# Fold in banks of its own, its last block and the narrow work among gate and up, down two blocks behind: an AdaLN-FFN pair on one core

## The chip, the cores and the metric

One core of a Trainium2 chip. The metric is the device time of one execution in microseconds; runs of a kernel are compared by their median.

## The reference

For eight blocks x[b] of 128 rows (e) by 512 columns:

```python
y = sum(x[b][:, :length[b]], axis=1) / length[b]          # per row
gate = sigmoid(conv5(y))                                  # along the 128 rows
a = x * gate                                              # each row scaled
h = silu(bitlinear(a, w_gate)) * bitlinear(a, w_up)       # 512 -> 1376
x = x + bitlinear(h, w_down)                              # 1376 -> 512
# bitlinear: rows rounded to int8 by their maximum, weights to -1, 0, 1 by mean |w|
w_eff = codebook_quantised(weight + delta) * scale + delta   # delta = lora_B @ lora_A / 2
c = x @ w_eff.T
x = x + c @ W_base.T + b_base + sum over 4 experts of alpha * (c @ A.T) @ B.T * 2
# alpha = softmax(log(prior) + router logits) over the active experts
```

## The kernel before

Each engine has its own hand-written queue, and semaphores join them. Blocks are numbered 0 to 7; F = 1376 is cut into chunks of 464, 464 and 448 columns.

*Weights of layer 1.* In four row blocks k: `normalise` adds delta, `masks` compares with seven thresholds (L955, VectorE), `codebook` multiplies masks by diagonal steps on TensorE (L660, L661), `value` and `w_eff` (L963, L970, VectorE) finish the block. `fold` (L672) multiplies w_eff by W_base into four banks, so that layer 1 needs one matrix M; `selection` (L642 to L648) gathers the active experts' A and router rows, `last_fold` (L694) multiplies w_eff by them (the narrow fold, 36 columns), `b_rows` (L679) gathers B. `m_high` (L501, ScalarE) and `m_low` (L1107, VectorE) split M into two parts.

*Weights of layer 0.* ScalarE sums absolute values (`weight_sum`, L451), TensorE adds over partitions (`weight_total`, L633), VectorE makes the scale (`weight_scale`, L998 to L1002), ScalarE rounds (`rounded_chunk` L480, `rounded_down` L518), VectorE clips (`ternary`, L1016).

*The gate of layer 0.* `x_sum` (L993, VectorE) for each block, the mean and taps (L1070, L1071), `conv` (L685, TensorE: five shifted matmuls, each in two passes), then exp on ScalarE (L506) and 1/(1 + exp) on VectorE for all eight blocks at once (L1090, L1091). `x_max` (L1020) and `x_scales` (L1079 to L1084) give the quantisation scales for a range of blocks, `x_quantise` (L1098) one block of integers, `x_transposes` (L723) and `x_evacuate` (L495) the operand of TensorE.

*A block.* `gate_up(b, c)` (L756) is eight matmuls into a pair of banks (4 and 5, or 6 and 7, in turn); `silu_chunk` (L528, ScalarE), `hidden_chunk` (L1138 and L1141, VectorE: product and maximum), after three chunks `hidden_scale` (L1145 to L1148), `hidden_round` (L535, ScalarE), `hidden_transposes` (L770), `hidden_evacuate` (L545, L547), `down` (L785, 11 matmuls into bank 2), `residual` (L1153, L1155, VectorE). The new x is transposed into bank 2 again by `x1_transposes` (L792) and split by `x1_high` (L555) and `x1_low` (L1160), after which bank 2 is free for the next down. TensorE's order is the loop

```python
gate_up(b, 0); x1_transposes(b - 2)      # b >= 3
gate_up(b, 1); hidden_transposes(b - 1)  # b >= 1
x_transposes(b + 1)
gate_up(b, 2); down(b - 1)               # b >= 2; down(0) earlier in block 2
```

and the tail: `layer1` groups (L834, 12 matmuls by the two parts of M and of x), the last downs and transposes between them, the router logits (L732 to L734), `z_rows` (L811), the softmax, and `experts` (L841). SP issues all loads in a fixed order, the down weight after the last codebook.

## Time and profile before

| | us |
|---|---|
| runs of the kernel | 160.44, 162.75, 162.95; median 162.75 |
| the profiled execution | 160.56 |
| its span, first to last instruction | 158.8 |
| mean granted TensorE clock | 0.979 |

The profile shows one execution. Starts in it are counted from the first instruction. A matmul's busy time includes its way through the array, so the busy times of neighbours overlap; the distance of their starts is the time that they take.

### The profile page before, as it was taken

The numbers are of one execution on the slowest core, as the hardware profiler recorded it, in microseconds if no ns is written. First come the engines' busy times: TensorE is split into PE (matmuls) and PEld (weight loads), VectorE is DVE, ScalarE is ACT, GpSimd is POOL, SyncE is SP. The second block draws the span as 40 slices with busy tenths as digits, with TensorE's granted clock in tenths as the row PEclk, the third lists the DMA queues.
The fourth block names the chain that finished last, engine by engine and source line by source line (L and its number), as shares of the span: only waits on it lengthen the run. The fifth ranks groups of instructions, "written<-read, shape, count | busy, mean of one in ns | idle before, by whom it ended". The sixth has DMA issues, their size and how long they took to land.

```text
span 158.8 us, 2289 instructions
## 1 busy us (share of the span) xinstructions
PE 146.0 (92%) x755; PEld 90.1 (57%) x762; DVE 114.3 (72%) x306; ACT 96.4 (61%) x160; POOL 3.2 (2%) x17
## 2 busy tenths in 40 slices
PE   6789999999988987597999999999999999999993
PEld 2256575766673444244454555556456857688782
DVE  2799999899699498979999777799777212026461
ACT  3899996968981979987184666767474401500200
POOL 7000000000000000000000000000000000000000
PEclk9999999999985799999999999999999999999999
DMA  5999999479100000000000000000000000000093
GB/s 174 350 405 418 403 418 400 192 261 400 53 0 0 0 0 2 4 0 0 0 4 0 0 0 0 6 0 0 2 0 4 0 0 0 0 4 0 17 378 133
DMA packets 6543, 15.99 MB, mean 101 GB/s; under 512 B 658, under 2 KB 914, under 8 KB 6532
## 3 DMA queue, kind: packets, MB, share of 16 engines
q1 hardware_dynamic: 6532, 15.85, 26.5%
q8 instruction: 6, 0.10, 0.3%
q14 instruction: 5, 0.04, 0.1%
HBM read 13.76 MB, written 2.10 MB: 100 GB/s over the span
## 4 chain that ended last, share of the span: by engine, by line
PE 74%; DVE 11%; ACT 6%; issue 5%; DMA 2%; SPq 0%; ACTq 0%; DVEq 0%
PE bank L756 16%; PE bank L834 14%; PE bank L785 10%; PE bank L672 9%; PE bank L660 4%; PE bank L661 4%; DVE raw_up L1138 3%; DMA cond<-in_cond_w 2%; PE bank L694 2%; PE bank L792 2%; DVE hmax L1141 2%; PE bank L770 2%; ACT tern_d L451 1%; PE bank L841 1%; PE bank L733 1%
## 5 line engine op out<-in xcount | busy, mean ns | idle before, releaser
L756 PE MATMUL bank<-tern_g,l1ab 128*128 128x464 bf16 (+1 forms) x96 | 24.1, 375 | 4.4 <-DVE raw_up L1138 1.7
L756 PE MATMUL bank<-tern_u,l1ab 128*128 128x464 bf16 (+1 forms) x96 | 23.6, 370 | 0.0
L834 PE MATMUL bank<-m_h,fr 128*128 128x512 f32 (+1 forms) x72 | 22.1, 376 | 0.0
L535 ACT ACTIVATE raw_up<-raw_up,hq 128x1376 int16<-128x1376 f32 x8 | 11.5, 1442 | 16.4 <-DVE hq L1148 16.4
L785 PE MATMUL bank<-tern_d,delta 128*128 128x512 bf16 (+1 forms) x81 | 18.8, 379 | 1.6 <-DVE fr L1160 1.0
L528 ACT ACTIVATE cond<-bank,s_g 128x464 f32<-128x464 f32 (+1 forms) x24 | 15.2, 638 | 8.0 <-PE bank L756 7.9
L1138 DVE TENSOR_TENSOR raw_up<-bank,cond 128x464 f32<-128x464 f32 (+1 forms) x24 | 15.2, 632 | 6.1 <-ACT cond L528 5.8
L756 PEld LDWEIGHTS bank<-tern_g,l1ab 128*128 128x128 bf16 x96 | 9.0, 101 | 13.6 <-ACT l1ab L495 4.4
L1141 DVE TENSOR_REDUCE hmax<-raw_up 128x1 f32<-128x464 f32 (+1 forms) x24 | 15.1, 631 | 0.8
L756 PEld LDWEIGHTS bank<-tern_u,l1ab 128*128 128x128 bf16 x96 | 9.8, 102 | 10.2 <-issue 1.6
L785 PEld LDWEIGHTS bank<-tern_d,delta 128*128 128x128 bf16 (+1 forms) x88 | 8.3, 98 | 11.7 <-DVE fr L1160 1.6
L834 PEld LDWEIGHTS bank<-m_h,fr 128*128 128x128 f32 x72 | 13.1, 188 | 2.7
L672 PE MATMUL bank<-wbt,cond 128*128 128x512 f32 x32 | 14.5, 595 | 0.0
L660 PE MATMUL bank<-masks,diag_h 128*128 128x512 f32 x28 | 12.4, 444 | 1.8 <-DVE masks L955 1.8
L834 PE MATMUL bank<-m_l,fr 128*128 128x512 f32 (+1 forms) x36 | 13.3, 369 | 0.0
L955 DVE TENSOR_SCALAR masks<-cond,th 128x512 fp32r<-128x512 f32 x28 | 11.7, 482 | 0.1
L547 ACT ACTIVATE delta<-bank 128x768 bf16<-128x768 int16 (+1 forms) x16 | 11.2, 700 | 0.5 <-PE bank L770 0.5
L661 PE MATMUL bank<-masks,diag_l 128*128 128x512 f32 x28 | 11.0, 395 | 0.0
L1155 DVE SCALAR_TENSOR_TENSOR xs<-bank,s_d,xs 128x512 f32<-128x512 f32 x8 | 6.0, 751 | 5.7 <-PE bank L785 5.5
L555 ACT ACTIVATE fr<-bank 128x512 fp32r<-128x512 f32 x8 | 4.7, 592 | 8.6 <-PE bank L792 8.6
L1160 DVE TENSOR_TENSOR fr<-bank,fr 128x512 fp32r<-128x512 f32 x8 | 5.5, 692 | 5.9 <-ACT fr L555 5.7
L672 PEld LDWEIGHTS bank<-wbt,cond 128*128 128x128 f32 x32 | 6.0, 190 | 6.4 <-issue 6.2
(168 smaller groups left out, 227.1 us busy)
## 6 DMA issues: line engine op xcount, KB each, us to landing
raw_gate<-in_w_gate_t SPq DMA_DIRECT2D x4, 688.0 KB, 8.2
raw_up<-in_w_up_t SPq DMA_DIRECT2D x4, 688.0 KB, 13.8
xs<-in_x SPq DMA_DIRECT2D x8, 256.0 KB, 11.8
...
```

Of the source, the lines that this page charges most:

```text
L528: act.activation(silu[:, n % 2, 0:w], bank_g[n % 2][:, 0:w], ACT.Silu, scale=s_g[:, b:b + 1]).then_inc(silu_done, 1)
L535: act.activation(h_i[:, b % 2, :], hbuf[b % 2], ACT.Copy, scale=hq[:, b:b + 1]).then_inc(hint_done, 1)
L547: act.activation(h_t[:, b % 2, j0:j1, :], src[:, 0:(j1 - j0) * P].rearrange("p (j e) -> p j e", e=P), ACT.Copy).then_inc(ht_done, 1)
L660: pe.matmul(bank_cb[k][:], diag_h[:, t, :], mask[i % SLOTS], start=(n == 0), stop=False)
L661: mm = pe.matmul(bank_cb[k][:], diag_l[:, t, :], mask[i % SLOTS], start=False, stop=(n == NT - 1))
L672: mm = pe.matmul(bank_m[k][:], cond[:, o, k * P:(k + 1) * P], wbt[:, o, :], start=(o == 0), stop=(o == KH - 1))
L756: mm = pe.matmul(dst[:, 0:w], xq_t[:, b % 2, k, :], w_t[:, k, f0:f0 + w], start=(k == 0), stop=(k == KH - 1))
L785: mm = pe.matmul(bank_down[:], h_t[0:rows, b % 2, j, :], tern_d[0:rows, j, :], start=(j == 0), stop=(j == KF - 1))
L834: pe.matmul(bank_y[n_res][:, h0:h1], a[:, b, k, :], m[:, k, h0:h1], start=(n == 0), stop=False)
L955: dve.tensor_scalar(mask[i % SLOTS], cond[:, k, :], t(T_ORDER[n]), None, ALU.is_gt)\
L1138: dve.tensor_tensor(hs, bank_u[n % 2][:, 0:w], silu[:, n % 2, 0:w], ALU.mult)\
L1141: link(dve.tensor_reduce(hmax[:, b % 2, c:c + 1], hs, AX.X, ALU.max, apply_absolute_value=True))
```

## The change

The four fold banks are now 0 to 3, apart from those of gate and up. The last block of the fold is done one bank at a time: bank 0, x transposes of block 0, bank 1, gate_up(0, 0) and (0, 1), banks 2 and 3. Selection stands after gate_up(0, 2), the narrow fold and the total of the down weight after gate_up(1, 2), the b rows in block 2. The banks of M are copied to SBUF (`m_copy`), and split in blocks 5 and 6. The x sums, taps and convolutions are done for blocks 0-1, 2-4 and 5-7 in turn, and the gate is silu(y)/y, with a stand-in where y is all but zero, which needs one table set of ScalarE for all of the layer. x and the x1 transposes leave bank 3 and bank 2 (x: bank 6 once, then the end of bank 1; x1: bank 3). down is two blocks behind gate and up, x1 transposes three. The scale of the residual is computed on GpSimd. The silu of a chunk waits for the gate half only. In TensorE's hidden transposes, eight parts go to the first bank and three to the second instead of six and five.

```diff
+GROUPS = [(0, 2), (2, 5), (5, NB)]
+CONV_WITH_XT = {1: 1, 4: 2}
 ...
+late = slice(HT_LATE * P, HT_LATE * P + H)
+bank_xT = [bank[6][:].bitcast(BF16)[:, 0:H]] + [bank_hT[1][:, late]] * (NB - 1)
+bank_xTi = [bank[6][:].bitcast(I16)[:, 0:H]] + [bank_hTi[1][:, late]] * (NB - 1)
+bank_x1T = bank[3]
+bank_zt = [bank[2], bank[1]]
 ...
-bank_m = [bank[6], bank[7], bank[0], bank[1]]
+bank_m = [bank[0], bank[1], bank[2], bank[3]]
 ...
-bank_delta = [bank[6], bank[7], bank[2], bank[3]]
+bank_delta = [bank[2], bank[3], bank[6], bank[7]]
 ...
-bank_sel = bank[2]
-bank_b = bank[5]
-bank_conv = bank[3][:, 0:NB]
-bank_total = [bank[3][:, 0:KH], bank[3][:, 0:KH], bank[1][:, 0:len(DOWN_PARTS)]]
+bank_sel = bank[3]
+bank_b = bank[3]
+conv0 = (HT_LATE * P + H) // 2
+bank_conv = [bank[6][:, conv0:conv0 + NB], bank[1][:, conv0:conv0 + NB], bank[1][:, conv0:conv0 + NB]]
 ...
-load_x(2)
-load_x(3)
 load_up(0)
 load_wbase(2)
 load_up(1)
+load_up(2)
 load_wbase(3)
-load_up(2)
 load_up(3)
-for b in range(4, NB):
+for b in range(2, 5):
     load_x(b)
 sp.dma_start(l1ab[:], lora1).then_inc(ld_exp, 16)
 sp.dma_start(b_full[3 * ZC:ZS, :], b_base).then_inc(ld_exp, 16)
+for b in range(5, NB):
+    load_x(b)
 ...
+pool.wait_ge(winv_done, 3)
+for b in range(NB):
+    pool.wait_ge(hscale_done, b + 1)
+    pool.tensor_scalar(s_d[:, b:b + 1], harow[:, b:b + 1], w127[:, 2:3], None, ALU.mult).then_inc(sd_done, 1)
 ...
+act.preload_act_table_set("silu_and_others")
 ...
+def conv_out(g):
+    b0, b1 = GROUPS[g]
+    act.wait_ge(conv_ps, g + 1)
+    act.activation(ycond[:, b0:b1], bank_conv[g][:, 0:b1 - b0], ACT.Copy).then_inc(ycond_done, 1)
+def gate_silu(g):
+    b0, b1 = GROUPS[g]
+    act.wait_ge(ysafe_done, g + 1)
+    act.activation(ysilu[:, b0:b1], ysafe[:, b0:b1], ACT.Silu).then_inc(ysilu_done, 1)
+def m_copy(k):
+    act.wait_ge(fold_ps, k + 1)
+    act.activation(m_full[:, k, :], bank_m[k][:], ACT.Copy).then_inc(mfull_done, 1)
 def m_high(k):
-    act.wait_ge(fold_ps, k + 1)
-    act.activation(m_h[:, k, :], bank_m[k][:], ACT.Copy).then_inc(mh_done, 1)
-for k in range(KH):
-    m_high(k)
-act.wait_ge(conv_ps, 1)
-act.activation(yexp[:], bank_conv, ACT.Exp, scale=-1.0).then_inc(yexp_done, 1)
+    act.wait_ge(mfull_done, k + 1)
+    act.activation(m_h[:, k, :], m_full[:, k, :], ACT.Copy).then_inc(mh_done, 1)
+weight_sum_up(0)
+weight_sum_up(1)
+weight_sum_up(2)
+rounded_chunk(0, 0)
+weight_sum_up(3)
+rounded_chunk(0, 1)
+conv_out(0)
+rounded_chunk(0, 2)
+gate_silu(0)
+rounded_chunk(1, 0)
+x_evacuate(0)
+rounded_chunk(1, 1)
+rounded_chunk(1, 2)
 def weight_sum_down(i):
 ...
-act.wait_ge(gu_ps, n + 1)
+act.wait_ge(gate_ps, n + 1)
 ...
+if half == 1 and b + 2 < NB:
+    act.wait_ge(xt_ps, b + 3)
 ...
-for b in range(NB + 2):
+for b in range(NB + 3):
     if b < NB:
         silu_chunk(b, 0)
     if b >= 3:
-        x1_high(b - 2)
-    if b == 0:
-        weight_sum_down(1)
+        x1_high(b - 3)
+    if b == 1:
+        gate_silu(1)
         weight_sum_down(2)
+    if b == 2:
         act.wait_ge(ms_ps, 1)
         act.activation(ms_h, bank_ms[:, 0:KH * ZL].rearrange("p (k c) -> p k c", k=KH),
                        ACT.Copy).then_inc(msh_done, 1)
-    if b == 1:
         rounded_down(0)
     if b < NB:
         silu_chunk(b, 1)
+    if b == 0:
+        weight_sum_down(0)
+        for k in range(KH):
+            m_copy(k)
     if 1 <= b <= NB:
         hidden_evacuate(b - 1)
-    if b + 1 < NB:
+    if 1 <= b < NB - 1:
         x_evacuate(b + 1)
-    if b == 1:
+        if b + 1 in CONV_WITH_XT:
+            conv_out(CONV_WITH_XT[b + 1])
+    if b == 2:
         rounded_down(2)
-    if b == 2:
-        x1_high(0)
     if b < NB:
         silu_chunk(b, 2)
     if b == 0:
+        x_evacuate(1)
+        conv_out(1)
+        weight_sum_down(1)
+    if b == 1:
         weight_sum_down(3)
         weight_sum_down(4)
-    if b == 1:
+    if b == 2:
         rounded_down(3)
         rounded_down(4)
+        act.wait_ge(b_ps, 1)
+        act.wait_ge(rows_done, 5)
+        act.activation(b_full[0:3 * ZC, :], bank_b[0:3 * ZC, :], ACT.Copy,
+                       scale=two_row[0:3 * ZC, :]).then_inc(b_full_done, 1)
+    if b == 3:
+        gate_silu(2)
+    if b in (5, 6):
+        m_high(2 * (b - 5))
+        m_high(2 * (b - 5) + 1)
     if b < NB:
         hidden_round(b)
 for half in range(2):
 ...
+else:
+    pe.wait_ge(sel_read, 2)
 ...
 pe.wait_ge(ld_exp, 32)
+pe.wait_ge(mfull_done, KH)
 ...
-def fold(o):
+def fold(o, k):
-for k in range(KH):
 ...
+mm = pe.matmul(bank_m[k][:], cond[:, o, k * P:(k + 1) * P], wbt[:, o, :],
+               start=(o == 0), stop=(o == KH - 1))
+if o == KH - 1:
+    mm.then_inc(fold_ps, 1)
 ...
 def b_rows():
-    pe.wait_ge(value_done, KH)
+    pe.wait_ge(wtot_read, 3)
 ...
-def conv():
-    pe.wait_ge(ymean_done, 1)
-    pe.wait_ge(wtot_read, 2)
+def conv(g):
+    pe.wait_ge(ymean_done, g + 1)
+    if g == 0:
+        pe.wait_ge(delta_done, KH)
+    b0, b1 = GROUPS[g]
 ...
 lora_delta(2)
 lora_delta(3)
 codebook(1)
-fold(0)
+for k in range(KH):
+    fold(0, k)
 codebook(2)
 weight_total(0, bank_total[0], KH)
-fold(1)
+for k in range(KH):
+    fold(1, k)
 codebook(3)
-fold(2)
+conv(0)
 weight_total(1, bank_total[1], KH)
-for k in range(KH + 1):
-    selection(k)
-b_rows()
-fold(3)
-conv()
+for k in range(KH):
+    fold(2, k)
 def x_transposes(b):
     pe.wait_ge(xq_done, b + 1)
     pe.wait_ge(ident_done, 2)
     if b == 0:
-        pe.wait_ge(yexp_done, 1)
+        pe.wait_ge(ycond_done, 1)
     else:
         pe.wait_ge(xt_done, b)
+    if b == 1:
+        pe.wait_ge(mfull_done, 2)
+    if b in CONV_WITH_XT:
+        conv(CONV_WITH_XT[b])
 ...
 if n == 0:
-    pe.wait_ge(b_full_done, 1)
-if n == 1:
-    pe.wait_ge(ml_done, 2)
+    pe.wait_ge(value_done, KH)
 if n >= 2:
     pe.wait_ge(silu_done, n - 1)
+for k in range(KH):
+    mm = pe.matmul(bank_g[n % 2][:, 0:w], xq_t[:, b % 2, k, :], tern_g[:, k, f0:f0 + w],
+                   start=(k == 0), stop=(k == KH - 1))
+mm.then_inc(gate_ps, 1)
+if n >= 2:
     pe.wait_ge(hmul_done, n - 1)
-for dst, w_t in ((bank_g[n % 2], tern_g), (bank_u[n % 2], tern_u)):
 ...
+for k in range(KH):
+    mm = pe.matmul(bank_u[n % 2][:, 0:w], xq_t[:, b % 2, k, :], tern_u[:, k, f0:f0 + w],
+                   start=(k == 0), stop=(k == KH - 1))
 mm.then_inc(gu_ps, 1)
 ...
 if b == 0:
     pe.wait_ge(msl_done, 1)
 else:
-    pe.wait_ge(x1l_done, b)
+    pe.wait_ge(x1_done, b)
 pe.wait_ge(ht_done, 3 * (b + 1))
 ...
 def x1_transposes(b):
     pe.wait_ge(x1_done, b + 1)
+if b == 0:
+    pe.wait_ge(b_full_done, 1)
+else:
+    pe.wait_ge(x1l_done, b)
 for k in range(KH):
-    mm = pe.transpose(bank_down[:, k * P:(k + 1) * P], xs[:, b, k * P:(k + 1) * P], ident)
+    mm = pe.transpose(bank_x1T[:, k * P:(k + 1) * P], xs[:, b, k * P:(k + 1) * P], ident)
 mm.then_inc(x1t_ps, 1)
 ...
+fold(KH - 1, 0)
+x_transposes(0)
+fold(KH - 1, 1)
 for b in range(NB):
     gate_up(b, 0)
     if b >= 3:
-        x1_transposes(b - 2)
+        x1_transposes(b - 3)
     gate_up(b, 1)
-    if b == 1:
-        pe.wait_ge(ml_done, KH)
-        weight_total(2, bank_total[2], len(DOWN_PARTS))
-    if b == 2:
-        down(0)
+    if b == 0:
+        fold(KH - 1, 2)
+        fold(KH - 1, 3)
     if b >= 1:
         hidden_transposes(b - 1)
-    if b + 1 < NB:
+    if 1 <= b < NB - 1:
         x_transposes(b + 1)
     if b == 2:
-        x1_transposes(0)
+        b_rows()
     gate_up(b, 2)
+    if b == 0:
+        x_transposes(1)
+        for k in range(KH + 1):
+            selection(k)
+    if b == 1:
+        for k in range(KH):
+            last_fold(k)
+        weight_total(2, bank_total[2], len(DOWN_PARTS))
     if b >= 2:
-        down(b - 1)
+        down(b - 2)
 last = NB - 1
 layer1(0)
-x1_transposes(last - 1)
+x1_transposes(last - 2)
+down(last - 1)
 hidden_transposes(last)
 layer1(1)
+x1_transposes(last - 1)
 down(last)
 layer1(2)
 ...
+def y_safe(g):
+    o = slice(*GROUPS[g])
+    dve.wait_ge(ycond_done, g + 1)
+    link(dve.tensor_tensor(ytiny[:, o], ycond[:, o], ycond[:, o], ALU.mult))
+    link(dve.tensor_scalar(ytiny[:, o], ytiny[:, o], TINY_SQUARE, STAND_IN, ALU.is_lt, ALU.mult))
+    dve.tensor_tensor(ysafe[:, o], ycond[:, o], ytiny[:, o], ALU.add).then_inc(ysafe_done, 1)
+    dve.wait_ge(ysafe_done, g + 1)
+    link(dve.reciprocal(yrec[:, o], ysafe[:, o]))
+def gates(g):
+    o = slice(*GROUPS[g])
+    dve.wait_ge(ysilu_done, g + 1)
+    link(dve.tensor_tensor(gate[:, o], ysilu[:, o], yrec[:, o], ALU.mult))
 ...
-dve.tensor_scalar(w127[:, i:i + 1], wscale[:, i:i + 1], 1.0 / QMAX, None, ALU.mult)
+link(dve.tensor_scalar(w127[:, i:i + 1], wscale[:, i:i + 1], 1.0 / QMAX, None, ALU.mult))
 ...
+weight_scale(0, bank_total[0])
 masks(3, 4)
 w_eff(2)
-weight_scale(0, bank_total[0])
 lengths()
-selectors()
 x_sum(0)
+x_sum(1)
+y_taps(0)
 ternary_chunk(0, 0, rounded_by_act=1)
+x_max(0, 2)
+ternary_chunk(0, 1, rounded_by_act=2)
 value(3)
+weight_scale(1, bank_total[1])
+y_safe(0)
+gates(0)
+x_scales(0, 2)
+x_quantise(0)
 w_eff(3)
-dve.wait_ge(lp_done, 1)
-dve.tensor_copy(pr_bc[:], pr.unsqueeze(2).broadcast_to([NE, 2, P])).then_inc(sel_done, 1)
-x_sum(1)
-ternary_chunk(0, 1, rounded_by_act=2)
+ternary_chunk(0, 2, rounded_by_act=3)
+ternary_chunk(1, 0, rounded_by_act=4)
 x_sum(2)
 x_sum(3)
-weight_scale(1, bank_total[1])
-ternary_chunk(0, 2, rounded_by_act=3)
+ternary_chunk(1, 1, rounded_by_act=5)
 x_sum(4)
-x_sum(5)
-dve.wait_ge(sel_ps, 1)
 ...
-ternary_chunk(1, 0, rounded_by_act=4)
-x_sum(6)
-x_sum(7)
 ...
-x_max(0, 1)
-ternary_chunk(1, 1, rounded_by_act=5)
 ...
-dve.wait_ge(yexp_done, 1)
-link(dve.tensor_scalar(yexp[:], yexp[:], 1.0, None, ALU.add))
-link(dve.reciprocal(gate[:], yexp[:]))
-x_scales(0, 1)
 ...
+y_taps(1)
 ...
-dve.tensor_tensor(m_l[:, k, :], bank_m[k][:], m_h[:, k, :].bitcast(F32),
+dve.tensor_tensor(m_l[:, k, :], m_full[:, k, :], m_h[:, k, :].bitcast(F32),
 ...
+dve.wait_ge(gu_ps, n + 1)
 ...
-link(dve.tensor_scalar(s_d[:, o], harow[:, o], w127[:, 2:3], None, ALU.mult))
+dve.wait_ge(sd_done, b + 1)
 ...
-    dve.tensor_tensor(x1t_l[:, b, :, :], bank_down[:].rearrange("p (k e) -> p k e", k=KH),
+    dve.tensor_tensor(x1t_l[:, b, :, :], bank_x1T[:].rearrange("p (k e) -> p k e", k=KH),
                       x1t_h[:, b, :, :].bitcast(F32), ALU.subtract).then_inc(x1l_done, 1)
-for b in range(NB + 2):
-    if b + 1 < NB:
+for b in range(NB + 3):
+    if b == 1:
+        selection_out()
+        y_safe(1)
+    elif b + 1 < NB:
         x_quantise(b + 1)
-    if b == 2:
-        residual(0)
     if b < NB:
         hidden_chunk(b, 0)
     if b == 0:
+        selectors()
+        dve.wait_ge(lp_done, 1)
+        dve.tensor_copy(pr_bc[:], pr.unsqueeze(2).broadcast_to([NE, 2, P])).then_inc(sel_done, 1)
+    if b == 1:
+        gates(1)
+        x_scales(2, 5)
+        x_quantise(2)
+    if b == 2:
+        weight_scale(2, bank_total[2])
         dve.wait_ge(msh_done, 1)
         dve.tensor_tensor(ms_l, bank_ms[:, 0:KH * ZL].rearrange("p (k c) -> p k c", k=KH),
                           ms_h.bitcast(F32), ALU.subtract).then_inc(msl_done, 1)
-    if b == 1:
         ternary_down(0)
     if b >= 3:
-        x1_low(b - 2)
+        x1_low(b - 3)
     if b < NB:
         hidden_chunk(b, 1)
+    if b == 0:
+        x_max(2, 5)
+    if b == 1:
+        x_sum(5)
     if b == 2:
-        x1_low(0)
-        x_scales(4, 6)
-    if b == 1:
         ternary_down(1)
         ternary_down(2)
     if b < NB:
         hidden_chunk(b, 2)
         hidden_scale(b)
-    if b == 0:
-        x_max(5, 6)
-        weight_scale(2, bank_total[2])
     if b == 1:
+        x_sum(6)
+        x_sum(7)
+        y_taps(2)
+    if b == 2:
         ternary_down(3)
         ternary_down(4)
-        x_max(4, 5)
-    if 2 <= b <= NB:
-        residual(b - 1)
-    if b == 2:
-        x_max(6, NB)
-        x_scales(6, NB)
-    if b == 5:
+        x_max(5, 7)
+    if b == 3:
+        y_safe(2)
+        x_max(7, NB)
+        gates(2)
+        x_scales(5, NB)
+    if 2 <= b <= NB + 1:
+        residual(b - 2)
+    if b in (5, 6):
+        m_low(2 * (b - 5))
+        m_low(2 * (b - 5) + 1)
+    if b == 7:
         stacked_b()
```

## Rows read from the trace of the kernel before

**Rows 1.** The page: its span, and busy us (share) xinstructions of each engine.
```profile
span 158.8 us, 2289 instructions
...
PE 146.0 (92%) x755; PEld 90.1 (57%) x762; DVE 114.3 (72%) x306; ACT 96.4 (61%) x160; POOL 3.2 (2%) x17
```

**Rows 2.** Busy time by stretch: stretch, us, busy (xcount) per engine, granted clock, DMA.
```profile
34.00:41.80 7.80, 7.80 (x34) 4.92 (x33) 7.45 (x24) 5.76 (x5) 0.00 (x0) 1.00 0.85 313
41.80:46.60 4.80, 4.80 (x47) 4.79 (x45) 3.49 (x13) 4.54 (x8) 0.00 (x0) 1.00 0.00 0
46.60:53.40 6.80, 5.45 (x18) 2.12 (x16) 6.26 (x14) 3.04 (x4) 0.00 (x0) 0.50 0.00 0
53.40:65.00 11.60, 8.50 (x57) 4.53 (x54) 8.86 (x22) 10.70 (x21) 0.00 (x0) 1.00 0.00 1
65.00:78.00 13.00, 11.29 (x64) 5.64 (x66) 11.36 (x29) 8.77 (x13) 0.00 (x0) 1.00 0.00 1
78.00:95.70 17.70, 17.34 (x108) 9.38 (x109) 15.12 (x37) 11.04 (x18) 0.00 (x0) 1.00 0.00 1
95.70:121.20 25.50, 25.12 (x156) 13.74 (x158) 20.76 (x47) 16.04 (x26) 0.00 (x0) 1.00 0.01 2
```

**Rows 3.** The chain that ended last, TensorE's pieces: start us, us, what.
```profile
31.01 3.43 PE bank L672 x8
34.56 0.25 PE bank L642 x2
...
37.50 1.03 PE bank L679 x2
...
41.97 1.01 PE bank L685 x10
42.98 3.60 PE bank L694 x32
...
48.24 3.27 PE bank L756 x8
...
87.15 1.57 PE bank L756 x8
88.74 0.66 PE bank L792 x4
...
90.96 0.61 PE bank L770 x11
91.58 0.22 PE bank L723 x4
...
93.36 2.32 PE bank L785 x10
95.69 1.57 PE bank L756 x8
```

**Rows 4.** Timeline of ScalarE: start us, us, line, operation [idle before, releaser].
```profile
30.78 3.51 ACT L480 ACTIVATE tern_i<-raw_gate,winv 128x1856 int16<-128x1856 f32 x2
...
51.53 0.65 ACT L528 ACTIVATE cond<-bank,s_g 128x464 f32<-128x464 f32 x1 [3.43 <-PE bank L756]
...
61.06 1.56 ACT L518 ACTIVATE tern_i<-raw_down,winv 128x1536 int16<-128x1536 f32 x1
```

**Rows 5.** Timeline of VectorE, same columns.
```profile
25.27 1.27 DVE L955 TENSOR_SCALAR masks<-cond,th 128x512 fp32r<-128x512 f32 x3
...
79.55 1.21 DVE L1020 TENSOR_REDUCE rmax<-xs 128x2 f32<-128x1024 f32 x1
80.80 0.16 DVE L1079 TENSOR_TENSOR arow<-rmax,gate 128x2 f32<-128x2 f32 x1
...
81.86 0.55 DVE L1098 TENSOR_SCALAR head_sb<-xs,gate,qx 128x512 int16<-128x512 f32 x1
82.32 0.63 DVE L1138 TENSOR_TENSOR raw_up<-bank,cond 128x464 f32<-128x464 f32 x1
...
83.66 0.69 DVE L1160 TENSOR_TENSOR fr<-bank,fr 128x512 fp32r<-128x512 f32 x1
```

More of the change, by code:

```diff
@@ L538, in hidden_evacuate @@
             def hidden_evacuate(b):
-                for half, (j0, j1) in enumerate(((0, 6), (6, KF - 1))):
+                for half, (j0, j1) in enumerate(((0, HT_EARLY), (HT_EARLY, KF - 1))):
                     act.wait_ge(ht_ps, 2 * b + half + 1)
@@ L761, in hidden_transposes @@
                 pe.wait_ge(hint_done, b + 1)
[L762 removed]
+                for half, (j0, j1) in enumerate(((0, HT_EARLY), (HT_EARLY, KF))):
                     if b == 0:
[L764 to L765 removed]
+                        pe.wait_ge(mfull_done, 2)
                     else:
```

136 lines of the change are left out of this document (62 added, 74 removed).

## The prediction

> **What bounds the kernel now.** I read the page first [rows 1]: TensorE is busy for 92% of a span of 158.8 us, so what can be won is mostly the time in which it waits or runs slowly. The busy times by stretch [rows 2] say where that is. From 95.7 to 121.2 us TensorE works 25.12 of 25.50 us and VectorE 20.76: there TensorE sets the pace. From 53.4 to 78 us it is idle for 3.1 + 1.71 us, and VectorE is as full (20.22 of 24.6 us): there TensorE waits for hidden chunks, quantised x and the ternary down weight. From 46.6 to 53.4 us the granted clock is 0.50, the lower level of 1.2 GHz, after 4.8 us in which TensorE did only narrow matmuls (8 and 36 columns), and it is idle for 1.35 us besides.
>
> The chain gives the price of each piece of TensorE's work [rows 3]: eight matmuls of a gate_up chunk 1.57 us (3.27 at the lower clock), down 2.32, hidden transposes 0.61, x transposes 0.22, x1 transposes 0.66, a fold of one block 3.43 (0.86 for one bank), one convolution 1.01, narrow fold 3.60, selection 2.94 (from 34.56 to 37.50), b rows 1.03. A block costs 8.54 us (from 87.15 to 95.69) when nothing waits.
>
> **What could be won.** From 31 us to the start of block 5 (95.69) TensorE is idle for 1.35 + 3.1 + 1.71 + 0.36 = 6.5 us [rows 2], and the lower clock costs 3.27 - 1.57 = 1.7 us on the first gate_up chunk and some 1.1 on the second [rows 3]: 9.3 us in all. The change moves the last fold, selection, narrow fold and b rows into this stretch, but doesn't shorten them. It adds two convolutions: ten matmuls each for three or fewer columns instead of eight. Below nothing they cannot be; the weight loads, not the columns, make their length, so I take the 1.01 us of the wide one for each (bounds 0.3 and 1.3), 2.0 us of new TensorE work.
>
> **The walk, block by block.** I lay the new order of each queue on the durations of before.
>
> *Up to the first gate_up.* VectorE ends value(2) at 25.27, where the masks start [rows 5]. New order: scale of gate 0.76 (one wait more than now), three masks 1.2, w_eff(2) 0.6, lengths 0.6, two x sums at 0.8, taps 0.3 (the small ones as they stand in the same timeline): 30.3. Ternary 0.55 and x maxima of two blocks 1.25 (79.55 to 80.80 [rows 5]): 32.1. ScalarE now also loads its silu table early (1.28 us), which pushes back its first rounded chunk from a start that waited for the weight scale to one that no longer does: it starts at 27.75 as it does now, so the load is free. The second rounded chunk ends at 32.6 as now (two of them take 3.51 from 30.78 [rows 4]). Then ternary 0.55, value(3) 0.66, scale of up 0.76, y_safe 0.8 (four small linked operations), gate 0.2, x_scales 1.06, x_quantise 0.46 [rows 5], and only then w_eff(3): 37.8. TensorE has done codebook(3) at 31.0, conv(0), the weight total and fold(2) at 35.7 [rows 3] and waits 2.2 us for w_eff(3). Fold, x transposes, evacuation (0.5): the first gate_up starts at 39.9 instead of 48.24. The second waits for a ternary chunk whose rounding ScalarE could begin only after the evacuation: 42.2, a stall of 0.75. The third rounded chunk of up ends at 43.1, and the first silu starts there, against 51.53 [rows 4]. So the head start is 8.4 us.
>
> *Block 0.* VectorE: quantise 0.46, three hidden chunks at 1.34 (82.32 to 83.66 [rows 5]), selectors and the copy behind them 1.2, maxima of three blocks 1.78, hidden scale 0.77: 51.9. TensorE does two banks of the last fold, gate_up, conv(1), transposes and selection by 51.2. ScalarE has copied the four banks by 47.7, in time for the selection.
>
> *Block 1.* Silu(1,0) stands behind hidden_round(0) on ScalarE, which starts at 51.9: 53.8. Then hidden chunk, gates, x_scales, x_quantise(2): 56.9. TensorE, through with the hidden transposes at 54.9, waits 2.1 us. gate_up(1,2) 58.8, narrow fold 62.4, total of the down weight 62.65. VectorE, with three x sums (2.4) and the taps among its chunks, is at 63.5.
>
> *Block 2.* gate_up(2,0) ends at 64.2, hidden chunk 65.7, scale of down 66.5 (in the kernel before, rounding of the down weight starts at 61.06 [rows 4]). ScalarE has waited 2.2 us for it. Rounding (1.46), silu, two evacuations, another rounding, silu(2,2): 71.8. VectorE ends that chunk and its scale at 73.9 and the last two ternary parts at 74.5. down(0) could have started at 69.0; it gets its parts at 71.4, 71.8, 74.3 and 74.5 and ends at 75.0 instead of 71.3: 3.7 us of stall.
>
> *Block 3.* Without a stall TensorE is through at 84.3. But VectorE can start hidden chunk (3,2) only at 82.1 (conv(2) stands ahead of its gate_up), and then has chunk 1.31, scale 0.77, y_safe 0.8, a maximum 0.7, gates 0.2, x_scales 1.06 and the residual 0.67 to do: 87.6. The x1 transposes of block 4 wait for that residual from 85.9 to 87.8, 1.9 us, with gate_up(4,1) queued behind them. Block 5 then starts at 94.5; small gaps between groups, which the chain has and this walk lacks, make it 95.05.
>
> **The sum.** That is 0.65 us ahead of 95.69. But down lags by one more block now: TensorE still owes one down and one set of x1 transposes, 2.32 + 0.62 = 2.9 us. From there on TensorE is the bound as before; m_high and m_low (four times 0.5 and 0.6 us) fit into blocks 5 and 6, where VectorE has 8.5 - 6.6 = 1.9 us to spare. The tail has the same pieces in the order x1 transposes, down, hidden transposes, and each wait lies beside a 2.8 us layer-1 group. Net: +2.3 us, a span of 161.1. Checked the other way: new stalls 2.2 + 0.75 + 2.1 + 3.7 + 1.9 = 10.7 us and convolutions 2.0, against 9.3 us of waits and slow clock that go, and 0.6 to 1.6 us of small gaps which those stalls swallow: +1.8 to +2.8.
>
> The profiled execution took 160.56 us for its span of 158.8; with 1.76 around it, 161.1 gives 162.9. The median of the runs is 162.75, two of the three being 2.2 to 2.4 above the profiled one. I add half of that, since I don't know whether what lengthens those is still there, and predict 164.0.
>
> **The clock, and the skill.** The trace has the clock at full through 34 to 41.8 us with selection in it (the profile's TensorE was busy throughout and wide folds followed), and at half after 4.8 us of narrow work alone [rows 2]. In the new order the longest narrow stretch is conv(1), x transposes and selection, 4.2 us, then the narrow fold, 3.6 us behind a stall; I count no fall in the sum. The Trainium skill ("Perfetto Trace Analysis", Matmul Optimizations) says that TensorE scales with its utilization and that matmuls should run back-to-back in batches. By it, narrow work between wide chunks is right, but the thin stretch under down(0) is wrong. The rule gives no price; the rows do, in the first rival.
>
> **Rivals.**
> 1. *The clock falls again*, in selection, in the narrow fold or while down(0) waits for its parts. For: the fall after 4.8 us of narrow work. Against: two stretches are shorter, and TensorE waits at 55 and 86 us anyway, which swallows part. Each chunk costs 1.7 us more; two or three of them, less what is swallowed: +1 to +3.5, a time of about 166.
> 2. *The head start carries through (faster).* VectorE has 5.0 us of idle time in the walk between 43.7 and 87.6 (0.85 in block 1, 0.9 and 1.25 in block 2, 2.0 in block 3), all of it waiting for orders of queues. If silu(1,0) and x_quantise(2) don't hang on hidden_round(0), the narrow fold and the scale of down come 2 us earlier, and down(0) loses its stall; the place is down(0)'s end: if it is before 71 us, the result is faster. All 5.0 us gained give 164.0 - 5.0 = 159.0, and with the slow clock of before gone from the other runs too, 157. Against: each wait stands written in the queues, and VectorE has some 5 us more to do after the first silu than before (x sums, selectors, maxima, gates).
> 3. *The extra idle is narrower than that, and all is even*: stalls of down(0) and block 4 come out at half, 2.8 us less: 161.2, no change to be seen.
>
> **How the numbers follow.** My walk 0.45 (it and rival 3 lie within 2%), rival 3 0.15, clock rival 0.22, head start 0.18. The range takes in half of the head start case and the clock case with its upper price: 158.0 to 168.0. A change of about 2%, 3.3 us, is what a measurement of this kernel can tell from none: faster means under 159.5, slower over 166.0. Faster 0.18 plus a little of rival 3 gives 0.2; slower most of the clock case and the upper part of the walk, 0.27; the rest 0.53.
>
> **What would show it.** Right: first gate_up near 40 us after an idle of some 2 us ended by w_eff; first silu near 43; TensorE idle near 55 to 57 ended by the quantised x; down(0) in pieces, ended by tern_d near 75; an idle of 1 to 2 us before the x1 transposes near 86, ended by VectorE; block 5 starting near 95; busy TensorE after it. Wrong: down(0) in one piece, block 5 starting before 92, a granted clock of 0.50 for over 3 us anywhere after 45, or waits in the tail between the layer-1 groups.

## The result, and the profile after

| | before | after |
|---|---|---|
| runs | 160.44, 160.45, 162.75, 162.95 us; median 161.6 | 166.95, 167.58, 169.26, 169.87 us; median 168.42 |
| ratio after / before | | 1.039, 95% interval 1.031 to 1.047 |
| profiled execution, its span | 160.56, 158.8 us | 166.95, 165.2 us |
| mean granted TensorE clock | 0.979 | 0.959 |

Medians are of all runs; the ratios and their intervals leave out runs more than 1.5% above the fastest of their kernel.

The changed kernel is slower by 3.9%. The forecast was 164.0 with a range of 158.0 to 168.0. That is 0.8% above the 162.75 it started from, and the prediction gave the larger chance, 0.53, to a change too small to be told from none, and 0.27 to a slower kernel. So the direction was right and the size was not: the profiled execution, 166.95, lies near the upper end of the range, the median of the runs 0.4 us above it.

The page of the changed kernel, its first lines:

```profile
span 165.2 us, 2369 instructions
...
PE 151.2 (92%) x775; PEld 94.6 (57%) x782; DVE 114.5 (69%) x308; ACT 99.7 (60%) x169; POOL 5.7 (3%) x25
...
PEclk9999999999997598799999689999999999999999
```

TensorE is busy 5.2 us longer than before (146.0 [rows 1]), VectorE 0.2 us. The clock row has three dents where the kernel before had one. Only TensorE's matmuls stretch with the clock: in the first dent four of them start 1.52 us after the four before (52.57 to 54.09) instead of 0.79 (40.59 to 41.38), while a silu of 464 columns takes ScalarE 0.65 us and a product of them VectorE 0.64 us inside the dent and outside. So the dents are the first thing to follow.

TensorE's timeline of the changed kernel (start us, us, line, operation [idle before, releaser]), the rows at which the walk of the prediction can be checked:

```profile
31.00 1.17 PE L741 MATMUL bank<-ytaps,shifts 128*128 128x2 f32 x10
32.03 0.36 PE L687 MATMUL bank<-wsum,ones 128*128 128x4 f32 x2
...
38.49 1.13 PE L726 MATMUL bank<-wbt,cond 128*128 128x512 f32 x2 [2.55 <-DVE cond L1042]
...
40.59 0.95 PE L808 MATMUL bank<-tern_g,head_sb 128*128 128x464 bf16 x4
...
43.01 0.96 PE L808 MATMUL bank<-tern_g,head_sb 128*128 128x464 bf16 x4 [0.69 <-DVE tern_u L1110]
...
52.57 1.73 PE L808 MATMUL bank<-tern_g,head_sb 128*128 128x464 bf16 x4
...
74.91 1.25 PE L842 MATMUL bank<-tern_d,delta 128*128 128x512 bf16 x5 [1.37 <-DVE tern_d L1110]
77.83 0.82 PE L842 MATMUL bank<-tern_d,delta 128*128 128x512 bf16 x3 [1.66 <-DVE tern_d L1110]
78.49 0.95 PE L808 MATMUL bank<-tern_g,head_sb 128*128 128x464 bf16 x4
...
91.63 0.66 PE L853 MATMUL bank<-shifts,xs 128*128 128x128 f32 x4 [2.03 <-DVE xs L1239]
...
100.09 0.95 PE L808 MATMUL bank<-tern_g,head_sb 128*128 128x464 bf16 x4
```

A convolution of two columns takes 1.03 us (31.00 to 32.03), as the one of eight did (1.01 [rows 3]). The wait for w_eff is there (2.55 us; forecast 2.2), the wait for the ternary chunk (0.69; 0.75), the pieces of down(0) (1.37 + 1.66 us of visible wait; forecast 3.7 from an earlier possible start), the wait of the x1 transposes for the residual (2.03; 1.9). The first gate_up starts at 40.59 instead of 48.24. But block 5 starts at 100.09, where the walk had 95.05. The wait for x of block 2, forecast at 2.1 us, is not there at all: TensorE came too late for it.

The stretches of the changed kernel, columns as in [rows 2]:

```profile
49.00:51.40 2.40, 2.40 (x19) 2.19 (x17) 2.33 (x3) 2.12 (x4) 0.00 (x0) 1.00 0.00 0
51.40:58.30 6.90, 6.90 (x21) 3.39 (x22) 4.21 (x19) 3.86 (x6) 0.00 (x0) 0.51 0.01 2
58.30:65.00 6.70, 6.70 (x61) 5.74 (x60) 5.84 (x17) 5.30 (x10) 0.00 (x0) 1.00 0.00 1
65.00:68.40 3.40, 3.40 (x11) 1.28 (x9) 1.87 (x7) 1.18 (x3) 0.00 (x0) 0.51 0.00 0
68.40:92.30 23.90, 18.73 (x117) 10.38 (x118) 19.11 (x49) 15.74 (x24) 1.35 (x4) 1.00 0.00 1
92.30:95.70 3.40, 3.40 (x16) 1.77 (x15) 2.05 (x4) 1.24 (x2) 0.00 (x0) 0.52 0.00 0
```

Three falls to the lower level of 1.2 GHz: one behind conv(1), x transposes and selection (6.9 us long), one behind the narrow fold (3.4), one behind the 2.03 us wait for the residual (3.4). Half of 13.7 us is 6.8 us of TensorE's work lost. In the kernel before TensorE worked for 5.45 of the 6.80 low microseconds [rows 2], so 2.7 us of its work were lost, and it had waits behind them that could take some of them up; here TensorE is busy for all of the low stretches.

### The profile page after: what moved, and what is told of

Same layout as the page of the kernel before. It is cut to its first block, busy times and chain, and to the rows that moved or that the text cites. A ratio compares the mean times of both kernels' runs of the same rounds, so it can differ in the third digit from the quotient of the medians.

```text
span 165.2 us, 2369 instructions
## 1 busy us (share of the span) xinstructions
PE 151.2 (92%) x775; PEld 94.6 (57%) x782; DVE 114.5 (69%) x308; ACT 99.7 (60%) x169; POOL 5.7 (3%) x25
## 4 chain that ended last, share of the span: by engine, by line
PE 70%; ACT 14%; DVE 10%; issue 5%; ACTq 0%; DVEq 0%
PE bank L895 13%; PE bank L808 11%; PE bank L814 11%; PE bank L842 9%; ACT tern_d L475 6%; PE bank L827 3%; PE bank L853 2%; PE bank L669 2%; ACT tern_i L505 2%; PE bank L749 2%; PE bank L666 2%; PE bank L726 2%; PE bank L902 1%; PE bank L741 1%; PE bank L782 1%
## 5 line engine op out<-in xcount | busy, mean ns | idle before, releaser
L808 PE MATMUL bank<-tern_g,head_sb 128*128 128x464 bf16 (+1 forms) x96 | 25.6, 394 | 0.7 <-DVE tern_u L1110 0.7
L814 PE MATMUL bank<-tern_u,head_sb 128*128 128x464 bf16 (+1 forms) x96 | 25.5, 393 | 0.0
L1222 DVE TENSOR_TENSOR raw_up<-bank,wbt 128x464 f32<-128x464 f32 (+1 forms) x24 | 15.2, 632 | 12.9 <-ACT wbt L568 9.2
L568 ACT ACTIVATE wbt<-bank,s_g 128x464 f32<-128x464 f32 (+1 forms) x24 | 15.3, 641 | 3.6 <-PE bank L808 3.5
L726 PE MATMUL bank<-wbt,cond 128*128 128x512 f32 x32 | 15.0, 603 | 2.6 <-DVE cond L1042 2.6
L814 PEld LDWEIGHTS bank<-tern_u,head_sb 128*128 128x128 bf16 x96 | 10.2, 107 | 11.6 <-issue 3.5
L808 PEld LDWEIGHTS bank<-tern_g,head_sb 128*128 128x128 bf16 x96 | 9.5, 105 | 10.7 <-issue 3.3
L589 ACT ACTIVATE delta<-bank 128x1024 bf16<-128x1024 int16 (+1 forms) x16 | 11.2, 701 | 7.3 <-PE bank L827 7.3
L1330 DVE TENSOR_TENSOR xs<-bank,xs 128x512 f32<-128x512 f32 (+1 forms) x9 | 5.2, 626 | 5.6 <-PE bank L902 5.6
```

The lines of the kernel that those rows point to most:

```text
L568: act.activation(silu[:, n % 2, 0:w], bank_g[n % 2][:, 0:w], ACT.Silu, scale=s_g[:, b:b + 1]).then_inc(silu_done, 1)
L589: act.activation(h_t[:, b % 2, j0:j1, :], src[:, 0:(j1 - j0) * P].rearrange("p (j e) -> p j e", e=P), ACT.Copy).then_inc(ht_done, 1)
L726: mm = pe.matmul(bank_m[k][:], cond[:, o, k * P:(k + 1) * P], wbt[:, o, :], start=(o == 0), stop=(o == KH - 1))
L808: mm = pe.matmul(bank_g[n % 2][:, 0:w], xq_t[:, b % 2, k, :], tern_g[:, k, f0:f0 + w], start=(k == 0), stop=(k == KH - 1))
L814: mm = pe.matmul(bank_u[n % 2][:, 0:w], xq_t[:, b % 2, k, :], tern_u[:, k, f0:f0 + w], start=(k == 0), stop=(k == KH - 1))
L1222: dve.tensor_tensor(hs, bank_u[n % 2][:, 0:w], silu[:, n % 2, 0:w], ALU.mult)\
```

## The experiments

Eleven kernels ran. Each is compared with the kernel before on the same chip, whose medians there were 162.2 to 162.7 us (160.5 to 164.1); so I give ratios beside times. The changed kernel was not run again beside them, so differences from its median of 168.42 are the rougher ones.

**Dense matmuls in three thin stretches.**

```diff
+def dense(dst, n):
+    for i in range(n):
+        pe.matmul(dst[:], warm[:, 0:P], warm[:], start=True, stop=True)
 for k in range(KH + 1):
     selection(k)
+    dense(bank[2], 1)
 ...
 for k in range(KH):
     last_fold(k)
+    dense(bank[3], 1)
 ...
 def x1_transposes(b):
+    if b == 1:
+        pe.wait_ge(x1l_done, 1)
+        dense(bank[3], 8)
     pe.wait_ge(x1_done, b + 1)
```

> The changed kernel with dense matmuls (512 bf16 columns, results unused) put between the narrow ones: one after each of the five selection steps, one after each of the four steps of the narrow fold, eight while TensorE waits for the residual of block 1. They cost 9 x 0.22 = 2.0 us of TensorE's time outside of waits, of which the wait for x of block 2 takes up half. Theory A (the slow clock behind the narrow stretches is what the change costs beyond its walk: three falls, 6.8 us of work lost to half speed, 5.0 after what waits swallow): no fall after 45 us, block 5 starts near 96 instead of 100.1, span near 161.5, 3 to 4 us less than the changed kernel. Theory B (the granted clock falls for reasons that have nothing to do with what TensorE does there, or the orders of the queues alone hold the time): the falls stay and the time is that of the changed kernel plus up to 2 us.

Median 168.02 us, ratio 1.040 (1.030 to 1.050): no gain. Neither theory as written. The falls did not stay where they were, nor go. The profile of this kernel in stretches:

```profile
36.00:39.00 3.00, 0.62 (x2) 0.38 (x3) 2.83 (x11) 1.55 (x1) 0.00 (x0) 1.00 1.05 400
39.50:43.50 4.00, 4.00 (x14) 1.45 (x12) 2.65 (x7) 3.73 (x3) 0.00 (x0) 0.57 0.23 76
...
53.00:57.00 4.00, 4.00 (x15) 1.94 (x15) 0.96 (x6) 2.23 (x4) 0.00 (x0) 0.57 0.02 4
...
73.00:77.00 4.00, 1.96 (x9) 0.51 (x6) 3.78 (x7) 4.00 (x8) 0.00 (x0) 1.00 0.00 0
77.00:84.50 7.50, 5.96 (x18) 2.86 (x19) 5.16 (x12) 3.77 (x5) 0.50 (x1) 0.54 0.01 2
```

The fall behind the residual's wait is gone. New ones stand behind the wait for w_eff(3) (TensorE busy for 0.62 of 3 us before it) and behind the pieces of down(0) (1.96 of 4 us), which the changed kernel's profiled execution had passed at full clock; one comes even behind selection with its five dense matmuls. I call a stretch thin in which TensorE has only narrow matmuls or waits. Over the two profiles the falls stand behind five of them: the wait for w_eff(3), selection, the narrow fold, the pieces of down(0) and the wait for the residual. Which of them brings a fall is not fixed.

**Residual ahead of the gate work of block 3.**

```diff
+if 2 <= b <= NB + 1:
+    residual(b - 2)
 if b == 3:
     y_safe(2)
     x_max(7, NB)
     gates(2)
     x_scales(5, NB)
-if 2 <= b <= NB + 1:
-    residual(b - 2)
```

> The changed kernel with residual(1) ahead of y_safe(2), the last maximum, gates(2) and x_scales(5, 8) on VectorE in block 3. Theory A (x1 transposes of block 4 wait for the residual because 2.9 us of other work stand ahead of it, and the third fall of the clock is the consequence of that wait): the 2.0 us wait at 90 us goes, the third fall with its 1.7 us goes too, minus 3 to 3.7 us. Theory B (what stood ahead of the residual is then late for the next block, since hidden_round(3) and x_quantise(5) wait for it): the wait moves to the hidden transposes of block 4 and the gain is under 1 us.

Median 165.06 us, ratio 1.012 (1.000 to 1.025), 3.4 us under the changed kernel's median. The wait is gone; the x1 transposes of block 4 follow gate_up at once:

```profile
91.68 0.95 PE L808 MATMUL bank<-tern_g,head_sb 128*128 128x464 bf16 x4
92.46 0.95 PE L814 MATMUL bank<-tern_u,head_sb 128*128 128x464 bf16 x4
93.25 0.60 PE L853 MATMUL bank<-shifts,xs 128*128 128x128 f32 x4
```

It did not return at the hidden transposes. Theory A for the wait. The profiled execution had four low stretches (from 9.5, 40, 54 and 77.5 us), none near 92, and took 167.35 us at a mean clock of 0.948, where the changed kernel took 167.58 at 0.949; the best run, 163.00 us, shows 0.979. So the gain of the median seems to go mostly with the clock, and how much of it the third fall is worth isn't shown.

**Scale of the down weight first.**

```diff
+if b == 2:
+    weight_scale(2, bank_total[2])
 if b < NB:
     hidden_chunk(b, 0)
 ...
 if b == 2:
-    weight_scale(2, bank_total[2])
```

> The changed kernel with the scale of the down weight ahead of the first hidden chunk of block 2 on VectorE (it waits there for 1.4 us anyway). Theory A (down(0) waits 3.0 us for its ternary parts because rounding begins at 69.75, 2.9 us after ScalarE was free): rounding begins near 67, down(0) loses 2 to 3 us of wait, block 3 starts at 76 instead of 78.5, and the time falls by 2 us. Theory B (down(0) waits because VectorE and ScalarE are full in block 2 whatever the order): under 0.7 us.

Median 163.45 us, ratio 1.009 (1.003 to 1.014): 5 us under the changed kernel's median, more than twice what theory A gave. The mechanism is as theory A had it, in ScalarE's and then TensorE's timeline:

```profile
66.83 1.58 ACT L558 ACTIVATE tern_i<-raw_down,winv 128x1536 int16<-128x1536 f32 x1 [0.49 <-DVE winv L1096]
```

```profile
72.00 1.25 PE L842 MATMUL bank<-tern_d,delta 128*128 128x512 bf16 x5 [0.28 <-DVE tern_d L1110]
74.91 0.82 PE L842 MATMUL bank<-tern_d,delta 128*128 128x512 bf16 x3 [1.66 <-DVE tern_d L1110]
```

Rounding begins 2.9 us sooner, down(0) ends 2.9 us sooner and waits 1.1 us less. The rest goes with the clock: two low stretches instead of three (51.5 and 89 us), 5.1 us lost instead of 6.8. At nearly the same mean clock the two kernels are 2.3 us apart (164.61 us at 0.958, the changed kernel 166.95 at 0.959; one run each), which is what theory A gave. So a scale of four small operations, moved into an idle gap of VectorE, is worth some 1.4% by itself.

**w_eff of the last block first.**

```diff
 value(3)
+w_eff(3)
 weight_scale(1, bank_total[1])
 ...
 x_quantise(0)
-w_eff(3)
```

> The changed kernel with w_eff(3) right behind value(3) on VectorE instead of behind the quantisation of block 0. Theory A (the first gate and up hang on the chain w_eff, fold, x transposes): the 2.55 us wait at 38.5 becomes one of some 0.5 us for the x transposes, the first gate_up comes 0.9 us sooner. Theory B (by block 5 the waits behind it have swallowed such a lead, as they have swallowed most of the 8 us that the change wins at the first gate_up): the time moves by less than 0.5 us though the lead is there at 40 us.

Median 166.03 us, ratio 1.023 (1.012 to 1.035). The wait of 2.55 us is now one of 1.91 us for the quantised x:

```profile
38.81 0.40 PE L782 MATMUL bank<-ident_b,head_sb 128*128 128x128 bf16 x4 [1.91 <-DVE head_sb L1138]
```

Theory A had 0.5: it forgot that the quantisation itself moves back by w_eff's 0.6. The second gate_up starts at 42.38 instead of 43.01: the lead is 0.63 us. The gain of 2.4 us between medians is more than that lead, and the profiled execution lost 5.1 us to the clock instead of 6.8, so this run can't tell theory B from A: the clock's steps are larger than the effect.

**The three together.**

> The changed kernel with the three reorderings together: w_eff(3) behind value(3), the scale of the down weight ahead of the first hidden chunk of block 2, residual(1) ahead of the gate work of block 3. Theory A (the waits written into the new queues, and the falls of the clock that thin stretches bring, are what the change costs): the single gains add up, about 0.6 + 3.5 + 2 us, a span near 160 and a time level with the kernel before (ratio 0.98 to 1.01). Theory B (they share one cover: each only moves the point at which VectorE holds everything): no more than the best of the three, ratio 1.005 or above.

(The edit is the last three diffs.) Median 160.30 us, ratio 0.988 (0.976 to 1.000). Theory A; the sum of the single gains to the medians (3.4 + 5.0 + 2.4 = 10.8) is not reached (8.1). That they share the clock's part would explain it, but no run shows it. The profiled execution (0.968) still fell behind selection and behind the narrow fold, 5.1 us lost.

**The three with dense matmuls in the narrow stretches.** (Two after each step of selection and of the narrow fold; the edit is that of the first experiment with 2 in place of 1 and without the third place.)

> e5_three with two dense matmuls (512 bf16 columns, results unused) after each step of selection and of the narrow fold: 9 x 2 x 0.22 = 3.9 us of TensorE's time, about 1 us of it inside a wait. Theory A (the narrow stretches bring the falls near 51 and 65 us): these two falls go, worth up to 5 us, so 1 to 2 us below e5_three. Theory B (the falls come from the waits): they stay, and the time is 2 to 3 us above e5_three.

Median 160.92 us, ratio 0.999 (0.994 to 1.004). No fall in the profile (mean clock 1.0, span 159.0); six of the ten runs show 1.0 and take 160.80 to 160.92, the other four 0.989. So the falls of the narrow stretches do go, theory A in the mechanism, but it had 1 to 2 us of gain, and at 3.9 us of added work nothing is won: buying the clock back with idle matmuls costs what it returns here.

**Dense matmuls in every thin stretch, order untouched.**

```diff
+pe.wait_ge(value_done, KH)
+dense(bank[4], 11)
 fold(KH - 1, 0)
 ...
+if b == 0 and j in (3, 8):
+    pe.wait_ge(ht_done, 4)
+    dense(bank[0], 7)
 if b == 0 and j in firsts:
```

(and two after each narrow step, eight before the residual's wait)

> The changed kernel, order untouched, with dense matmuls in every thin stretch: eleven in the wait for w_eff(3), two after each narrow step, seven in each of the two long waits of down(0), eight in the wait for the residual. Outside of waits they cost 3.9 us less the 1 to 2 us that the wait for x of block 2 takes. In the first experiment falls came at 39.5, 53 and 77 us instead of 51, 65 and 92, each behind one of these stretches. Theory A (any of the five thin stretches can bring a fall, which of them do varies from execution to execution, and the total is what they have in common): no fall at all, a span of 161.1 (the walk at full clock) + 2.5 = 163.5, and less spread between runs. Theory B (the clock falls whatever is put there): falls of 3 to 7 us remain and the time is 169 or more.

Median 165.66 us, ratio 1.025 (1.017 to 1.034); three of the four runs lie at 165.47 to 165.70 us with a mean clock of 1.0, the fourth at 169.39 with 0.969. Theory A, and close in numbers: a span of 163.9 us against 163.5. Here, unlike in the kernel with the three reorderings, padding does pay: the median is 2.8 us under the changed kernel's, though the intervals of the two ratios just overlap. The fourth run shows that padding everything doesn't keep every fall away.

This is the measurement that separates the two parts of the loss. TensorE's timeline of this kernel, and one row of ScalarE's:

```profile
38.63 1.12 PE L730 MATMUL bank<-wbt,cond 128*128 128x512 f32 x2 [0.19 <-DVE cond L1056]
...
55.27 0.65 ACT L568 ACTIVATE wbt<-bank,s_g 128x464 f32<-128x464 f32 x1 [0.92 <-PE bank L812]
...
59.38 0.40 PE L786 MATMUL bank<-ident_b,head_sb 128*128 128x128 bf16 x4 [1.19 <-DVE head_sb L1152]
...
92.08 0.66 PE L863 MATMUL bank<-shifts,xs 128*128 128x128 f32 x4 [0.30 <-DVE xs L1253]
...
98.87 0.95 PE L812 MATMUL bank<-tern_g,head_sb 128*128 128x464 bf16 x4
```

The wait for x of block 2 is there again, 1.19 us; the forecast was 2.1. If the missing 0.9 us are dense work that the wait took up, the dense matmuls cost 3.9 - 0.9 = 3.0 us, and without them and without falls the span would be 163.9 - 3.0 = 160.9 us. That estimate leans on the forecast. One from rows alone: the dense matmuls in selection make ScalarE wait 0.92 us for block 1's first gate bank, so the x behind it comes that much later; those in the narrow fold stretch it from 3.72 us in the changed kernel (60.95 to 64.67) to 5.12 (61.13 to 66.25), by 1.4; and the waits that hold the others are still open by 0.15 to 0.40 us, so those cost nothing. That makes 163.9 - 2.3 = 161.6 us. The walk had 161.1, between the two.

It also says what the order is worth by itself. This kernel and the one before it have the same padding in the narrow stretches and differ in the three reorderings; in runs without a fall they take 165.47 to 165.70 and 160.80 to 160.92 us. At full clock the three reorderings are worth 4.8 us.

**The narrow work taken apart.**

```diff
 gate_up(b, 0)
+if b == 1:
+    for k in range(KH + 1):
+        selection(k)
+if b == 2:
+    last_fold(2)
 ...
 gate_up(b, 1)
+if b == 2:
+    last_fold(3)
 ...
 if b == 0:
     x_transposes(1)
-    for k in range(KH + 1):
-        selection(k)
 if b == 1:
-    for k in range(KH):
-        last_fold(k)
+    last_fold(0)
+    last_fold(1)
     weight_total(2, bank_total[2], len(DOWN_PARTS))
```

(on top of the three; VectorE's and ScalarE's copies behind them move to match)

> e5_three with the narrow work taken apart: selection behind gate_up(1,0), so that the convolution and the x transposes don't adjoin it, and the four steps of the narrow fold two behind gate_up(1,2), one behind gate_up(2,0), one behind gate_up(2,1). No work is added. Theory A (what counts is how long the narrow work runs unbroken): fewer or shorter falls before 70 us, 1 to 3 us below e5_three, and below the kernel before. Theory B (the order is worth nothing, the falls are the waits'): the same as e5_three within 1 us.

Median 158.81 us, ratio 0.983 (0.976 to 0.990), all four runs between 158.56 and 159.11: faster than both kernels. Theory A. One low stretch is left, behind a wait of 1.90 us for the quantised x of block 0, and down(0) has only one long wait:

```profile
39.00:43.00 4.00, 4.00 (x11) 1.36 (x10) 3.53 (x11) 4.00 (x4) 0.00 (x0) 0.57 0.33 113
43.00:73.00 30.00, 26.89 (x178) 17.68 (x176) 26.54 (x77) 25.65 (x43) 1.02 (x3) 1.00 0.00 1
73.00:94.00 21.00, 20.83 (x135) 12.09 (x134) 17.33 (x41) 12.34 (x22) 0.62 (x3) 1.00 0.00 1
```

Beside the clock, spreading also lets the total of the down weight go two steps of the narrow fold (1.8 us) sooner. This run doesn't tell the two apart, but the runs of the three together hint at the clock: the one with 0.987 took 158.36 us, no more than the 158.56 to 159.11 here at 0.989, and those with 0.978 and 0.968 took 159.96 to 161.41. The gain would then be that all four runs here keep more of the clock.

**The kernel before with dense matmuls in its narrow fold.**

```diff
 for k in range(KH):
     for o in range(KH):
         mm = pe.matmul(bank_ms[:, k * ZL:(k + 1) * ZL], cond[:, o, k * P:(k + 1) * P],
                        sel_f[:, o, :], start=(o == 0), stop=(o == KH - 1))
+    dense(bank[4], 2)
```

> The kernel before with two dense matmuls (512 bf16 columns, results unused) after each of the four steps of the narrow fold: 8 x 0.22 = 1.7 us of added work on TensorE. In the profile of before the clock is at half from 46.6 to 53.4 us, behind the convolution and the narrow fold. Theory A (that fall costs the kernel before little, since TensorE waits for VectorE at 55 to 65 us anyway): no fall, and the same time within 1 us, mean clock 1.0 instead of 0.97 to 0.98; the change's comparison is then with a kernel that loses little to the clock. Theory B (it loses its full 3.4 us): 1.7 us below before.

Median 162.09 us, ratio 1.001 (0.995 to 1.006): theory A, the same time. The fall behind the narrow fold is gone (nothing is low after 30 us). Three of the ten runs show a mean clock of 1.0 and take 160.40 to 160.55 us, as the best runs of before do at 0.978 (160.49 to 160.54 on this chip). So that fall cost the kernel before no more than the dense work costs.

The spread between runs stayed, and the profiled execution (0.988) shows a fall that the profile of before doesn't have:

```profile
9.50:13.50 4.00, 4.00 (x11) 3.14 (x12) 3.96 (x12) 4.00 (x13) 0.00 (x0) 0.57 1.04 420
```

It stands in the first codebook work, behind waits of 1.02 and 0.59 us, long before anything that the change moves. The matmuls behind it start at 13.86 us instead of 12.27, and the first gate_up at 51.24 instead of 48.24, 1.6 us of it by this fall.

**One block of lag again.**

```diff
 gate_up(b, 1)
+if b == 3:
+    down(1)
+if b == 4:
+    x1_transposes(2)
 ...
 if b >= 2:
-    down(b - 2)
+    down(0 if b == 2 else b - 1)
```

(on top of the kernel with the narrow work apart; residuals, x1 highs, lows and the tail to match)

> e8_three_spread with down one block behind again: down(0) at the end of block 2 as there, down(1) in the middle and down(2) at the end of block 3, down(b-1) from then on, x1 transposes to match. Theory A (the second block of lag is what lets down(0) come late without holding residuals and hidden chunks of blocks 3 and 4 together): VectorE and TensorE collide in blocks 3 and 4, 1 to 3 us above e8_three_spread. Theory B (the lag is neutral, one down and one set of x1 transposes only stand elsewhere, and the prediction's 2.9 us are a debt that is paid in the tail either way): within 0.7 us of e8_three_spread.

Median 161.77 us, ratio 1.002 (0.996 to 1.007), 3.0 us above the same kernel with a lag of two. Theory A, at its upper end. In block 4 TensorE now waits for x1_low(1), which stands behind VectorE's gate work and two hidden chunks:

```profile
91.71 0.63 PE L856 MATMUL bank<-shifts,xs 128*128 128x128 f32 x4 [2.63 <-DVE fr L1254]
```

The lag of two, which the prediction carried as a debt of 2.9 us, pays here: with a lag of one the rest of the change, reordered and spread, is level with the kernel before. Part of the 3.0 us could be due to where I put the moved pieces; another order of them was not tried.

**Dense matmuls inside the waits that are left.** (Seven ahead of the x transposes of block 0, six before the part of down(0) that waits.)

> e8_three_spread with dense matmuls inside its two longest waits, where they cost nothing: seven (1.5 us) before the x transposes of block 0, which wait 1.9 us, and six (1.3 us) before the part of down(0) that waits 1.6 us. Theory A (its one remaining fall, from 39 to 43 us, comes from the wait before it): fewer runs with a fall, mean clock nearer to 1.0, 0.5 to 1.5 us below e8_three_spread. Theory B (a fall there is swallowed, since the second gate_up waits for a ternary chunk then): the same time within 0.5 us.

Median 158.96 us, ratio 0.987 (0.983 to 0.991): theory B. Two of its four runs show a mean clock of 1.0 and the other two 0.989, and they lie within 0.5 us of each other (158.67 and 158.90; 159.02 and 159.17). One fall costs this kernel little. But it isn't the one that the theories speak of: nothing is low near 39 us any more, and the profiled execution fell behind selection, which stands there in one piece of 2.9 us:

```profile
54.00:58.00 4.00, 4.00 (x25) 2.53 (x23) 3.71 (x13) 2.29 (x5) 0.00 (x0) 0.57 0.01 4
```

So dense matmuls inside a wait did away with the fall behind it, and narrow work between wide chunks can still bring one.

## Why the prediction was right or wrong

*The walk.* Right nearly to the row: first gate_up 40.6 (39.9), wait for w_eff 2.55 (2.2), first silu 43.78 (43.1), down(0) in pieces, wait for the residual 2.03 (1.9), and TensorE busy afterwards. With the clock held up the span is 160.9 to 161.6 us by the two estimates above, against 161.1. So the part of the forecast by which the change wins 8.4 us at the first gate_up and gives it all back in waits, convolutions and the later down stands. Its three largest waits were each a matter of order, since moving one operation shortened each of them. One small step was off: the early table load is not free. It takes 1.28 us, and ScalarE's first rounded chunk starts at 28.15 us, 0.46 later than before, though its scale was ready at 26.15.

*The clock.* This is the step that failed: "I count no fall in the sum", with a rival that gave "+1 to +3.5" a chance of 0.22. Measured: three falls and 6.8 us of work lost, of which the profiled execution's span felt 3.6 to 4.3 us (165.2 against 161.6 or 160.9), a little more than the rival's upper price. Block 5 starts 5.0 us after the walk's (100.09 against 95.05); the rest of these 5.0 us is the walk's own error up to there, and it was made good by the next step, the lag, being put too high. That the walk's end came out so near is luck in part.

Two mistakes stand behind the clock. I judged each narrow stretch alone and found it a little shorter than the one that had brought the fall before, though there were now more of them: the profile of before fell at one place, those of the change and of the first experiment together at five. And I took waits of TensorE as something that swallows the loss; only the pieces of down(0) stood in the rival as a cause. But waits bring falls themselves: one stands behind the 2.03 us wait in the changed kernel, another behind the wait for w_eff(3) in the first experiment.

The Trainium skill ("Perfetto Trace Analysis", Matmul Optimizations) advises running matmuls back-to-back in batches and gives no number. The first experiment's profile agrees for down(0): 0.54 behind its pieces, from 77 to 84.5 us. The changed kernel's own profile has 1.00 there (68.4 to 92.3 us). And where the prediction took narrow work between wide chunks to be right, the trace shows 0.51 behind it, from 51.4 us.

*The share from the runs' spread.* I added 1.1 us because two runs of before lay above the profiled one, without knowing why. The spread goes with the clock. The runs of before on the chip of the last experiments fall into steps by their mean granted clock: 160.5 to 161.6 us at 0.978 or 0.979, 162.1 to 163.3 at 0.967 or 0.968, 163.9 at 0.958. Padding its narrow fold took one fall out of all of them and left the steps, 160.4 to 160.6 us at 1.0, 162.0 to 162.3 at 0.988 or 0.989, 163.9 at 0.979. So what the runs differ in are other falls; one of them was seen at 9.5 us. The same falls can come in the changed kernel, whose unprofiled runs show 0.949 to 0.938.

*The lag.* Putting the down and the x1 transposes still owed at 2.9 us overrated the lag a little. From block 5 to the end it was 65.1 us (165.2 - 100.1) against 63.1 before (158.8 - 95.7), so 2.0. A full block is 8.30 us instead of 8.54, the x1 transposes taking 0.44 instead of 0.66 with a bank of their own, and that over three blocks makes most of the difference:

```profile
100.25 0.78 PE bank L808 x4
101.82 0.44 PE bank L853 x4
...
108.55 0.79 PE bank L808 x4
```

(the chain of the changed kernel). And the prediction didn't see that the lag relieves blocks 3 and 4, worth 3.0 us in the reordered kernel.

*The rivals.* The faster one, "the head start carries through", named down(0)'s end before 71 us as its mark and 157 to 159 as its time. The changed kernel ended down(0) at 78.5. The reordered and spread kernel ended it at 73.7 and runs in 158.8 us: part of the head start can be kept, but not in the order that the change chose.

*How the 8 us divide.* Between the medians of the changed kernel and of the three reorderings lie 8.1 us. At full clock, both padded, the order is worth 4.8 of them; by that estimate some 3.3 us are falls that the better order no longer has or feels.

*What stays open.* Which of the thin stretches brings a fall in a given execution. Where the unprofiled runs fell is not recorded either.
